# A macaron block's FFN on one Trainium2 core: the mask of picks is transposed by a DMA and multiplied in by VectorE, instead of being added in PSUM by TensorE

## Chip, cores and metric

One Trainium2 chip, one NeuronCore of it. The metric is the time of one execution of the whole program, in microseconds (us): the median of several runs.

## What is computed

The input x is 32 x 512 rows of 256 numbers (16384 rows, 128 tiles of 128 rows). Three layers follow each other, each with a residual: a sparse FFN, an attention layer (gated slot attention), and the same FFN with the same weights again. The change is in the FFN:

```python
lr = xf @ m1                                          # 256 -> 64
mask_logits = jnp.einsum('bl,lxy->bxy', lr, m2) + mb  # 16 groups of 64
quant_mask = jnp.argmax(mask_logits, axis=-1)         # one pick per group
w = w1p[j, quant_mask]
mid = jnp.einsum('ai,aji->aj', xf, w)                 # the picked column of each group
relu = jax.nn.relu(mid)
v = w2p[j, quant_mask]
res = jnp.einsum('ai,aij->aj', relu, v) + b2
x = x + 0.5 * res
```

xf is the layer norm of x. The kernel does not gather weights: it computes all 1024 products of the row, sets those that were not picked to zero, and multiplies all 1024 by w2.

## The kernel before

The program is three phases: FFN, attention, FFN. Each goes over 128 tiles of 128 rows. Every engine has its own hand-written list of stages; a stage comes with an offset, and in step s of a phase the engine does stage (f, o) for tile s + o. So the list of an engine is its order within a step, and instructions of an engine run strictly in that order. The phases overlap by a few steps. The first phase also computes the attention's four projections of x1, the FFN's output (tiles s - 5), and its layer norm (tiles s - 2 and s - 3).

For an FFN tile t the work goes like this (names as in the code, lines of the kernel before):

- VectorE takes the row's mean and variance (L237, L245), GpSimd makes 1/sqrt and x minus mean (`centre`: L249, L254, L256), ScalarE the high f16 half of the normalized row (`high`, L265), VectorE the low half (`low`, L270). Numbers are carried as a high and a low f16 half, and three matmuls stand for one product.
- SP issues the DMA transpose of both halves into `ffn_xT_hl` (`turn`, L281).
- TensorE: `low_rank` makes the 64 low-rank numbers (L472, 6 matmuls of 128 columns), ScalarE (`low_high`, L562 and L563) and VectorE (`low_low`, L628) split them, TensorE's `mask_logits` makes 1024 logits per row, rows on partitions, in banks 1 and 2 (L678, L680).
- VectorE: `first_max` is a running maximum within each group of 64 (L601), `reached` marks the positions where it has reached the group's maximum (L606, into `step`), `reject` compares neighbours of `step` and gives `unpicked`, 1 where a column was not picked, rows on partitions (L615).
- TensorE: `up` makes mid transposed, the 1024 columns on partitions in 8 blocks of 128, rows along the free dimension (L700, 48 matmuls of 128 columns, banks 3 and 4 or 5 and 6). `pick` (L712, 8 matmuls of 128 columns) multiplies `unpicked` by `far_ident`, a diagonal of -2^40, and adds it to the same banks: this transposes the mask and drives what was not picked far below zero.
- ScalarE: `mid_high` is the relu of those banks, rounded to f16 (L556). VectorE: `mid_low` is max(mid, 0) minus that, from PSUM (L622). TensorE: `down` multiplies both halves by w2 (L472, 24 matmuls of 256 columns). VectorE: `finish` adds the residual (L637); GpSimd has added half of b2 to it (`add_bias`, L541); SP stores it (L505).

The orders within a step, with the tile offset in brackets:

```python
# first phase
PE:      up 0, pick 0, project_vf -5, low_rank 2, mask_logits 1, project_qk -5, down -1
VectorE: finish -2, norm.stats 5, norm2.stats -2, low_of_x1 -3, both aggregates, norm.low 4,
         mid_low 0, low_low 2, first_max 1, reached 1, reject 1
ScalarE: norm.high 4, norm2.high -3, mid_high 0, scale_vf -5, low_high 2, swish -5
# third phase
PE:      mask_logits 1, low_rank 2, up 0, pick 0, down -1
VectorE: finish -2, stats 5, low_low 2, first_max 1, reached 1, aggregate 5, low 4, reject 1, mid_low 0
ScalarE: high 4, low_high 2, mid_high 0
```

GpSimd does add_bias -1, centre 5 and, in the first phase, norm2.centre -2. SP issues load 6, load_residual 0, store -2, turn 3 and, in the first phase, norm2.turn -4 and store_projected -6; its queue is in order, and a wait of one entry holds those behind it. `low_of_x1` is norm2's low half, the scalar_tensor_tensor of L270 that writes `att_xn_hl`. The output of `down` and the low-rank numbers share bank 0 in the first phase, so `down` of tile t - 1 also waits for `low_low` of tile t + 2.

## Time and profile before

| | us |
|---|---|
| median of 3 runs | 3081.52 (3077.74 to 3081.72) |
| profiled execution, its own time | 3076.98 |
| span of its profile | 3075.2 |
| TensorE busy | 2976.7 (97% of the span) |
| VectorE busy | 2602.5 (85%) |
| ScalarE busy | 1419.7 (46%) |
| GpSimd busy | 1259.9 (41%) |

Busy time is that of compute instructions. PE is TensorE, DVE is VectorE, ACT is ScalarE, POOL is GpSimd, SPq is SP's queue of DMA issues. In a timeline each line is one instruction (or several of one kind in a row) with its start, its duration and, in square brackets, how long its engine had been idle and for whom. Two instructions in a row of VectorE or ScalarE overlap by about 0.1 us in these lines, so the spacing of starts says what one costs its engine. "PEclk" is the share of full speed that TensorE's clock was granted.

### The profile page before, as it was taken

The page shows a single profiled execution, that of the slowest core. Times are in us where ns is not written, and L with a number is a line of the kernel's source. Part 1 is how long each engine was busy: PE and PEld are TensorE (multiplying, and loading weights), DVE is VectorE, ACT ScalarE, POOL GpSimd, SP SyncE. Part 2 cuts the span into 40 slices and gives each one's busy share as a digit, 9 for nine tenths or more (in the row PEclk, how much of TensorE's full clock was granted, in tenths as well). Part 3 has the DMA queues.
Part 4 walks back from the last instruction along what each step waited for, and adds up shares of the span by engine and source line. Part 5 has one row for each costly group of instructions (what it writes and reads, how often), then busy time and mean ns, then how long its engine had stood idle before and what let it go on. Part 6 is the DMA issues. An engine that isn't in the chain of part 4 may idle for free.

```text
span 3075.2 us, 97305 instructions
## 1 busy us (share of the span) xinstructions
PE 2976.7 (97%) x34688; PEld 2609.5 (85%) x34688; DVE 2602.5 (85%) x4369; ACT 1419.7 (46%) x4051; POOL 1259.9 (41%) x2168
## 2 busy tenths in 40 slices
PE   5999999999999999799999999999899999999999
PEld 4888888888888888688888888888788888888888
DVE  8888888888888887488888888888899999999998
ACT  3333333333333333788888888887222222222222
POOL 4333333333333333255555555555433333333332
PEclk9999999999999999999999999999999999999999
DMA  4444444444444443444444444444332222222222
GB/s 111 119 124 125 125 124 124 124 123 123 123 123 123 123 123 115 126 129 132 133 132 135 133 132 131 131 133 127 92 77 75 75 75 75 76 77 77 76 77 58
DMA packets 485055, 340.86 MB, mean 111 GB/s; under 512 B 301940, under 2 KB 451828, under 8 KB 484984
## 3 DMA queue, kind: packets, MB, share of 16 engines
q1 hardware_dynamic: 484984, 339.91, 39.0%
q8 instruction: 46, 0.75, 0.1%
q14 instruction: 25, 0.20, 0.0%
HBM read 155.19 MB, written 117.44 MB: 89 GB/s over the span
## 4 chain that ended last, share of the span: by engine, by line
PE 93%; issue 2%; DVE 2%; ACT 1%; POOL 0%; DMA 0%; DVEq 0%; SPq 0%; POOLq 0%; ACTq 0%
PE banks L472 37%; PE banks L700 22%; PE banks L1196 7%; PE banks L1167 5%; PE banks L712 4%; PE banks L1192 4%; PE banks L680 3%; PE banks L678 3%; PE banks L1230 3%; PE banks L1157 2%; PE banks L1251 1%; PE banks L1283 1%; DVE masked L1052 1%; PE banks L1245 1%; DVE att_x_out L1134 0%
## 5 line engine op out<-in xcount | busy, mean ns | idle before, releaser
L700 PE MATMUL banks<-ffn_xT_hl,w_hl 128*128 128x128 f16 x12288 | 730.1, 219 | 0.0
L472 PE MATMUL banks<-w_hl,midT_hl 128*128 128x256 f16 x6144 | 712.6, 273 | 6.1 <-DVE low_hl L628 5.5
L700 PEld LDWEIGHTS banks<-ffn_xT_hl,w_hl 128*128 128x128 f16 x12288 | 704.5, 98 | 3.9 <-issue 0.6
L556 ACT ACTIVATE midT_hl<-banks 128x1024 f16<-128x1024 f32 x256 | 261.9, 1023 | 903.8 <-PE banks L712 903.8
L472 PEld LDWEIGHTS banks<-w_hl,midT_hl 128*128 128x128 f16 x6144 | 594.8, 98 | 75.9 <-DVE midT_hl L622 7.3
L249 POOL TENSOR_TENSOR ffn_var_eps<-ffn_moments,eps_col 128x1 f32<-128x1 f32 x256 | 94.1, 367 | 1270.7 <-DVE ffn_moments L245 1270.7
L601 DVE TENSOR_TENSOR_SCAN runmax<-restart,banks 128x1024 f32<-128x1024 f32 x256 | 585.4, 2287 | 8.8 <-PE banks L680 1.0
L622 DVE SCALAR_TENSOR_TENSOR midT_hl<-banks,midT_hl 128x1024 f16<-128x1024 f32 x256 | 312.6, 1221 | 193.8 <-ACT midT_hl L556 193.8
L606 DVE TENSOR_TENSOR step<-runmax 128x1024 bf16<-128x1024 f32 x256 | 314.8, 1230 | 8.9
L472 PE MATMUL banks<-wqkfv_hl,att_xT_hl 128*128 128x512 f16 (+1 forms) x1536 | 292.2, 326 | 1.5 <-DMA att_xT_hl<-att_xn_hl 1.5
L265 ACT ACTIVATE ffn_xn_hl<-ffn_xc,ffn_rstd 128x256 f16<-128x256 f32 x256 | 129.3, 505 | 307.7 <-POOL ffn_xc L256 292.1
L678 PE MATMUL banks<-m_high,low_hl 128*128 128x512 f16 x512 | 195.5, 382 | 2.9 <-DVE runmax L601 1.8
L472 PEld LDWEIGHTS banks<-wqkfv_hl,att_xT_hl 128*128 128x128 f16 x1536 | 139.7, 98 | 68.6 <-DMA att_xT_hl<-att_xn_hl 1.8
L541 POOL TENSOR_TENSOR x_res<-x_res,half_b 128x256 f32<-128x256 f32 x256 | 185.4, 724 | 26.4 <-DMA x_res<-x 25.9
L680 PE MATMUL banks<-m_low_mb,low_h 128*128 128x512 f16 x512 | 195.6, 382 | 0.0
L254 POOL TENSOR_TENSOR ffn_rstd<-ffn_var_eps,minus_half 128x1 f32<-128x1 f32 x256 | 184.1, 719 | 26.9 <-POOL ffn_var_eps L249 13.4
L615 DVE TENSOR_TENSOR unpicked<-step 128x1024 bf16<-128x1024 bf16 x256 | 180.4, 705 | 7.0
L472 PEld LDWEIGHTS banks<-ffn_xT_hl,m_hl 128*128 128x128 f16 x1536 | 107.9, 99 | 84.0 <-ACT w_hl L397 12.9
L994 ACT ACTIVATE prob<-logit,minus_top 128x64 f32<-128x64 f32 x512 | 171.9, 336 | 12.0 <-DVE minus_top L1067 5.1
L573 ACT ACTIVATE qkvf_out<-banks 128x512 f32<-128x512 f32 x128 | 76.5, 598 | 192.2 <-PE banks L472 192.2
L712 PE MATMUL banks<-far_ident,unpicked 128*128 128x128 bf16 x2048 | 156.6, 219 | 4.8 <-DVE unpicked L615 4.8
L1052 DVE TENSOR_TENSOR masked<-banks,causal 128x1024 f32<-128x1024 f32 (+1 forms) x130 | 156.8, 1206 | 0.7 <-PE banks L1167 0.7
(137 smaller groups left out, 5765.2 us busy)
## 6 DMA issues: line engine op xcount, KB each, us to landing
projected<-qkvf_out SPq DMA_DIRECT2D x128, 512.0 KB, 2.9
qkv<-projected SPq DMA_DIRECT2D x128, 384.0 KB, 3.3
x_in<-in_L_attn_x SPq DMA_DIRECT2D x128, 128.0 KB, 2.7
x_res<-in_L_attn_x SPq DMA_DIRECT2D x128, 128.0 KB, 2.1
x<-x_out SPq DMA_DIRECT2D x128, 128.0 KB, 2.0
gate<-projected SPq DMA_DIRECT2D x128, 128.0 KB, 3.1
att_x_res<-x SPq DMA_DIRECT2D x128, 128.0 KB, 2.1
x<-att_x_out SPq DMA_DIRECT2D x128, 128.0 KB, 1.7
```

The costliest lines, as they stand in the source:

```text
L472: last = nc.tensor.matmul(dst, left(lp, k), right(rp, k), start=(k == 0 and lp == rp), stop=(k == blocks - 1 and lp == 1))
L541: nc.gpsimd.tensor_tensor(x_res[:, t.slot], x_res[:, t.slot], half_b2[:, :], ALU.add).then_inc(res_biased, 1)
L556: nc.scalar.activation(midT_hl[:, t.slot, 0], mid_ps[t.slot], ACT.Relu).then_inc(mid_high_made, 1)
L601: nc.vector.tensor_tensor_scan(runmax[:, :], restart[:, :], logits_ps[:, :], FLOOR, ALU.add, ALU.max).then_inc(runmax_made, 1)
L606: nc.vector.tensor_tensor(step[:, :, 1:d2 + 1], groups, groups[:, :, d2 - 1:d2].broadcast_to([P, GROUPS, d2]), ALU.is_equal).then_inc(step ...
L622: nc.vector.scalar_tensor_tensor(midT_hl[:, t.slot, 1], mid_ps[t.slot], 0.0, midT_hl[:, t.slot, 0], ALU.max, ALU.subtract).then_inc(mid_lo ...
L678: nc.tensor.matmul(logits_ps[:, cols], low_hl[:, t.slot], m2_high2[:, cols], start=True, stop=False)
L680: last = nc.tensor.matmul(logits_ps[:, cols], low_h1[:, t.slot], m2_low_mb[:, cols], start=False, stop=True)
L700: nc.tensor.matmul(mid_ps[t.slot][:, cols], w1_hl[:, wp, k, cols], xT_hl[:, t.ring, xp, k], start=(c % PER_BANK == 0 and k == 0 and wp == xp),
L712: last = nc.tensor.matmul(mid_ps[t.slot][:, cols], unpicked[:, t.slot, cols], far_ident[:, :], start=False, stop=True, skip_group_check=True)
L1052: nc.vector.tensor_tensor(masked[:, t.slot, :, which].rearrange("p z b (a t) -> p z (b a) t", a=PAIRS), pair_ps[:, :, which].rearrange("p ...
L1196: last = nc.tensor.matmul(dst[:, at:at + HD], inner[:, z, a * P:(a + 1) * P], right[:, at:at + HD], start=(t.chunk == 0), stop=True, skip_ ...
```

## The change

`pick`, `far_ident` and `unpicked` go. `reject` becomes `pick_first`, which makes `picked` (1 where a column is picked) for the same tile. A new stage of SP, `turn_picked`, transposes it by DMA: 128 x 1024 bf16 into `pickedT`, 8 blocks of 128 x 128, where `turn` does 4. A new stage of VectorE, `cut`, makes `mid_cut` = max(mid, 0) * pickedT, 1024 columns of f32 in SBUF. `mid_high` becomes a copy of `mid_cut` to f16 on ScalarE, and `mid_low` (mid_cut minus its high half) moves from VectorE to GpSimd, at offset -1 and first in GpSimd's step. `up` raises `up_done`, for which `turn` of tile t + 4 and `cut` wait.

```diff
+                def turn_picked(t):
+                    if isinstance(t.n, int):
+                        after(sp, picked_made, t)
+                        after(sp, cut_made, t, lag=2)
+                    sp.dma_start_transpose(pickedT[:, t.slot], picked[:, t.slot]).then_inc(pick_turned[t.slot], 16)
...
-                              (load_residual, 0), (store, -2),
-                              (lambda t: norm.turn(sp, t, mid_picked), 3), (first_only(load_down, sp), 3),
+                              (load_residual, 0), (store, -2), (turn_picked, 0),
+                              (lambda t: norm.turn(sp, t, up_done), 3), (first_only(load_down, sp), 3),
...
-                              (lambda t: norm.turn(sp, t, mid_picked), 3)]
+                              (turn_picked, 0), (lambda t: norm.turn(sp, t, up_done), 3)]
...
-                stages = [(add_bias, -1), (lambda t: norm.centre(pool, t), 5)]
+                def mid_low(t):
+                    after(pool, mid_high_made, t)
+                    nc.gpsimd.tensor_tensor(midT_hl[:, t.slot, 1].rearrange("p c t -> p (c t)"), mid_cut[:, t.slot],
+                                            midT_hl[:, t.slot, 0].rearrange("p c t -> p (c t)"),
+                                            ALU.subtract).then_inc(mid_low_made, 1)
+                stages = [(mid_low, MID_LOW), (add_bias, -1), (lambda t: norm.centre(pool, t), 5)]
...
                 def mid_high(t):
-                    after(act, mid_picked, t)
+                    after(act, cut_made, t)
                     after(act, res_done, t, lag=2)
-                    nc.scalar.activation(midT_hl[:, t.slot, 0], mid_ps[t.slot], ACT.Relu
-                                         ).then_inc(mid_high_made, 1)
+                    nc.scalar.activation(midT_hl[:, t.slot, 0].rearrange("p c t -> p (c t)"), mid_cut[:, t.slot],
+                                         ACT.Copy).then_inc(mid_high_made, 1)
...
-                              (mid_high, 0), (scale_vf, -5), (low_high, 2), (first_only(round_down, act), 2),
-                              (swish, -5), (first_only(round_attention, act), -1)]
+                              (scale_vf, -5), (low_high, 2), (first_only(round_down, act), 2),
+                              (swish, -5), (mid_high, 0), (first_only(round_attention, act), -1)]
...
-                def reject(t):
+                def pick_first(t):
                     after(dve, step_made, t)
-                    after(dve, mid_picked, t, lag=2)
+                    after_dma(dve, pick_turned, t, lag=2)
                     nc.vector.tensor_tensor(
-                        unpicked[:, t.slot].rearrange("p (g d) -> p g d", g=GROUPS),
+                        picked[:, t.slot].rearrange("p (g d) -> p g d", g=GROUPS),
                         step[:, :, 0:d2], step[:, :, 1:d2 + 1],
-                        ALU.is_ge).then_inc(unpicked_made, 1)
-
-                def mid_low(t):
-                    after(dve, mid_high_made, t)
-                    nc.vector.scalar_tensor_tensor(midT_hl[:, t.slot, 1], mid_ps[t.slot], 0.0,
-                                                   midT_hl[:, t.slot, 0], ALU.max,
-                                                   ALU.subtract).then_inc(mid_low_made, 1)
+                        ALU.is_lt).then_inc(picked_made, 1)
+
+                def cut(t):
+                    after(dve, up_done, t)
+                    after_dma(dve, pick_turned, t)
+                    after(dve, mid_low_made, t, lag=2)
+                    nc.vector.scalar_tensor_tensor(mid_cut[:, t.slot], mid_ps[t.slot], 0.0,
+                                                   pickedT[:, t.slot].rearrange("p c t -> p (c t)"), ALU.max,
+                                                   ALU.mult).then_inc(cut_made, 1)
...
-                              (first_only(rest_of_up, dve), 3), (mid_low, 0), (low_low, 2), (first_max, 1),
-                              (reached, 1), (reject, 1), (first_only(rest_of_down, dve), 1),
+                              (first_only(rest_of_up, dve), 3), (low_low, 2), (first_max, 1),
+                              (reached, 1), (cut, 0), (pick_first, 1), (first_only(rest_of_down, dve), 1),
...
-                          (lambda t: norm.low(dve, t), 4), (reject, 1), (mid_low, 0)]
+                          (lambda t: norm.low(dve, t), 4), (cut, 0), (pick_first, 1)]
...
-                    after(pe, mid_low_made, t, lag=2)
+                    after(pe, cut_made, t, lag=2)
...
-                    stages = [(up, 0), (pick, 0), (project_vf, -5), (low_rank, 2), (mask_logits, 1),
+                    stages = [(up, 0), (project_vf, -5), (low_rank, 2), (mask_logits, 1),
                               (project_qk, -5), (down, -1)]
                 else:
-                    stages = [(mask_logits, 1), (low_rank, 2), (up, 0), (pick, 0), (down, -1)]
+                    stages = [(mask_logits, 1), (low_rank, 2), (up, 0), (down, -1)]
```

ScalarE in the first phase's loop, before (`mid_high` is L556, `swish` L573, `scale_vf` L581, `low_high` L562 and L563):

```order
L265 ACTIVATE att_xn_hl<-att_xc,att_rstd 128x256 [waits att_xT_turned2]
L556 ACTIVATE midT_hl<-banks 128x1024 [waits res_done,mid_picked]
L57 ISA [waits vf_projected]
L581 ACTIVATE qkvf_out<-banks 128x512 [waits qkvf_stored0]
L562 ACTIVATE low_hl<-banks 128x128 [waits logits_done,low_done]
L563 ACTIVATE low_h<-banks 64x128
L573 ACTIVATE qkvf_out<-banks 128x512 [waits qk_projected]
```

The same place in the changed kernel (its lines: `high` L263, `scale_vf` L590, `low_high` L571 and L572, `swish` L582, `mid_high` L565):

```order
L263 ACTIVATE att_xn_hl<-att_xc,att_rstd 128x256 [waits att_xT_turned2]
L57 ISA [waits vf_projected]
L590 ACTIVATE qkvf_out<-banks 128x512 [waits qkvf_stored0]
L571 ACTIVATE low_hl<-banks 128x128 [waits logits_done,low_done]
L572 ACTIVATE low_h<-banks 64x128
L582 ACTIVATE qkvf_out<-banks 128x512 [waits qk_projected]
L565 ACTIVATE midT_hl<-mid_cut 128x1024 [waits res_done,cut_made]
```

`mid_high` has moved from near the step's start to its end, and waits for VectorE's `cut` instead of TensorE.

VectorE in the third phase's loop, before, from `reached` (L606) to the next step's `low_low` (L628):

```order
L606 TENSOR_TENSOR step<-runmax 128x16x64 [waits runmax_made]
L245 BN_AGGR ffn_moments<-ffn_stats 128x2
L51 REGISTER_ALU
L270 SCALAR_TENSOR_TENSOR ffn_xn_hl<-ffn_xc,ffn_rstd,ffn_xn_hl 128x256 [waits ffn_xn_high_made]
L615 TENSOR_TENSOR unpicked<-step 128x1024 [waits mid_picked,step_made]
L622 SCALAR_TENSOR_TENSOR midT_hl<-banks,midT_hl 128x1024 [waits mid_high_made]
L637 SCALAR_TENSOR_TENSOR x_out<-banks,x_res 128x256 [waits out_stored1,res_biased,res_done]
L57 ISA [waits ffn_var_eps_made,ffn_centred]
L237 BN_STATS ffn_stats<-x_in 128x6 [waits ffn_x_loaded0]
L628 TENSOR_TENSOR low_hl<-banks,low_hl 64x128 [waits low_high_made]
```

The same in the changed kernel (`reached` L615, `cut` L633, `pick_first` L624, `finish` L648, `low_low` L639):

```order
L615 TENSOR_TENSOR step<-runmax 128x16x64 [waits runmax_made]
L243 BN_AGGR ffn_moments<-ffn_stats 128x2
L51 REGISTER_ALU
L268 SCALAR_TENSOR_TENSOR ffn_xn_hl<-ffn_xc,ffn_rstd,ffn_xn_hl 128x256 [waits ffn_xn_high_made]
L633 SCALAR_TENSOR_TENSOR mid_cut<-banks,pickedT 128x1024 [waits mid_low_made,pick_turned0,up_done]
L624 TENSOR_TENSOR picked<-step 128x1024 [waits pick_turned1,step_made]
L648 SCALAR_TENSOR_TENSOR x_out<-banks,x_res 128x256 [waits out_stored1,res_biased,res_done]
L57 ISA [waits ffn_var_eps_made,ffn_centred]
L235 BN_STATS ffn_stats<-x_in 128x6 [waits ffn_x_loaded0]
L639 TENSOR_TENSOR low_hl<-banks,low_hl 64x128 [waits low_high_made]
```

`cut` stands where `reject` stood, `pick_first` where `mid_low` stood; `cut` waits for a DMA, and what comes after it on ScalarE is given in the list of stages above: high 4, low_high 2, mid_high 0, unchanged in this phase.

## Rows read from the trace of the kernel before

**Rows 1.** The page, part 1: busy us, share of the span, instructions.
```profile
PE 2976.7 (97%) x34688; PEld 2609.5 (85%) x34688; DVE 2602.5 (85%) x4369; ACT 1419.7 (46%) x4051; POOL 1259.9 (41%) x2168
```

**Rows 2.** Windows view: stretches of the first and the third phase.
```profile
core 0: us, PE busy (x) PEld busy (x) DVE busy (x) ACT busy (x) POOL busy (x), PEclk, DMA share, GB/s
100.00:1100.00 1000.00, 1000.00 (x11929) 840.70 (x11928) 811.65 (x1258) 348.95 (x730) 365.36 (x733) 1.00 0.43 123
2250.00:3050.00 800.00, 800.00 (x10363) 713.85 (x10362) 769.47 (x1033) 223.53 (x459) 284.64 (x458) 1.00 0.28 75
```

**Rows 3.** Timeline of the first phase: start us, us, then the instruction.
```profile
801.08 0.61 PE L712 MATMUL banks<-far_ident,unpicked 128*128 128x128 bf16 x8
...
804.11 0.29 DVE L628 TENSOR_TENSOR low_hl<-banks,low_hl 64x128 f16<-64x128 f32 x1
804.44 2.29 DVE L601 TENSOR_TENSOR_SCAN runmax<-restart,banks 128x1024 f32<-128x1024 f32 x1
...
806.03 0.50 ACT L265 ACTIVATE ffn_xn_hl<-ffn_xc,ffn_rstd 128x256 f16<-128x256 f32 x1
806.43 0.50 ACT L265 ACTIVATE att_xn_hl<-att_xc,att_rstd 128x256 f16<-128x256 f32 x1
806.76 1.23 DVE L606 TENSOR_TENSOR step<-runmax 128x1024 bf16<-128x1024 f32 x1
...
810.64 0.61 PE L712 MATMUL banks<-far_ident,unpicked 128*128 128x128 bf16 x8
```

**Rows 4.** Timeline of the attention phase: GpSimd and VectorE side by side.
```profile
1803.76 0.73 POOL L919 TENSOR_TENSOR Pt<-prob,expG 128x256 f32<-128x256 f32 x1 [0.31 <-ACT prob L994]
...
1804.06 0.72 DVE L1126 TENSOR_TENSOR o_hl<-o_norm,o_hl 128x256 f16<-128x256 f32 x1
...
1804.45 0.85 POOL L900 TENSOR_TENSOR gate_hl<-logsig,gate_hl 128x256 f16<-128x256 f32 x1
...
1804.90 0.68 DVE L1036 SCALAR_TENSOR_TENSOR St<-keep,expnG 128x256 f32<-128x256 f32 x1
...
1808.32 1.01 POOL L928 TENSOR_TENSOR o_rms<-o_sum_eps,minus_half 128x4 f32<-128x4 f32 x1
...
1808.98 0.43 DVE L1027 SCALAR_TENSOR_TENSOR logsig<-gate,lnone 128x256 f32<-128x256 f32 x1 [0.23 <-ACT lnone L951]
```

**Rows 5.** Source view of the attention's GpSimd lines: ns min/median/max.
```profile
L900 POOL TENSOR_TENSOR gate_hl<-logsig,gate_hl x128: 664/673/859, 1249.1 to 2136.8; 128x256 f16<-128x256 f32 x128
L924 POOL TENSOR_TENSOR o_sum_eps<-o_sum,eps_sum_col x128: 196/198/203, 1296.4 to 2170.9; 128x4 f32<-128x4 f32 x128
```

**Rows 6.** Timeline of the third phase, one step and the next one's start.
```profile
2605.95 0.42 DVE L637 SCALAR_TENSOR_TENSOR x_out<-banks,x_res 128x256 f32<-128x256 f32 x1
...
2606.89 0.29 DVE L628 TENSOR_TENSOR low_hl<-banks,low_hl 64x128 f16<-64x128 f32 x1 [0.19 <-ACT low_hl L562]
...
2607.51 1.19 SPq L281 DMA_TRANSPOSE ffn_xT_hl<-ffn_xn_hl  x1
...
2609.71 1.02 ACT L556 ACTIVATE midT_hl<-banks 128x1024 f16<-128x1024 f32 x1 [2.69 <-PE banks L712]
...
2611.15 0.70 DVE L615 TENSOR_TENSOR unpicked<-step 128x1024 bf16<-128x1024 bf16 x1
...
2611.77 1.22 DVE L622 SCALAR_TENSOR_TENSOR midT_hl<-banks,midT_hl 128x1024 f16<-128x1024 f32 x1
...
2612.90 0.41 DVE L637 SCALAR_TENSOR_TENSOR x_out<-banks,x_res 128x256 f32<-128x256 f32 x1
...
2613.00 0.51 ACT L265 ACTIVATE ffn_xn_hl<-ffn_xc,ffn_rstd 128x256 f16<-128x256 f32 x1 [2.27 <-POOL ffn_xc L256]
...
2613.53 0.28 ACT L562 ACTIVATE low_hl<-banks 128x128 f16<-128x128 f32 x1
...
2613.84 0.29 DVE L628 TENSOR_TENSOR low_hl<-banks,low_hl 64x128 f16<-64x128 f32 x1 [0.19 <-ACT low_hl L562]
```

**Rows 7.** Tile view of ffn_xT_hl, 2300 to 3050 us: its transposes' landing.
```profile
DMA to landing us min/median/max: 2.4/2.6/4.0
```

More of the change, by code:

```diff
@@ L125, in build @@
     FLOOR = -3.0e38
-    FAR_BELOW = -(2.0 ** 40)
     S_ATT = 64.0
@@ L155, in bank @@
             return banks[:, first * BANK:(first + count) * BANK]
-        far_ident = sb("far_ident", [P, P], bf16)
         w1_hl = sb("w1_hl", [P, 2, KD, d_ff], f16)
@@ L185, in build @@
         runmax = sb("runmax", [P, d_ff])
-        unpicked = sb("unpicked", [P, 2, d_ff], bf16)
+        picked = sb("picked", [P, 2, d_ff], bf16)
+        pickedT = sb("pickedT", [P, 2, KF, P], bf16)
+        mid_cut = sb("mid_cut", [P, 2, KF * P])
         midT_hl = sb("midT_hl", [P, 2, 2, KF, P], f16)
@@ L699, in up @@
                             for wp, xp in ((0, 0), (0, 1), (1, 0)):
-                                nc.tensor.matmul(mid_ps[t.slot][:, cols], w1_hl[:, wp, k, cols],
-                                                 xT_hl[:, t.ring, xp, k],
-                                                 start=(c % PER_BANK == 0 and k == 0 and wp == xp),
-                                                 stop=False, skip_group_check=True)
-                def pick(t):
-                    if is_first(t) and in_first:
-                        pe.wait_ge(ident_made, 1)
-                    after(pe, unpicked_made, t)
-                    for c in range(KF):
-                        cols = slice(c * P, (c + 1) * P)
-                        last = nc.tensor.matmul(mid_ps[t.slot][:, cols], unpicked[:, t.slot, cols],
-                                                far_ident[:, :], start=False, stop=True,
-                                                skip_group_check=True)
-                    last.then_inc(mid_picked, 1)
+                                last = nc.tensor.matmul(mid_ps[t.slot][:, cols], w1_hl[:, wp, k, cols],
+                                                        xT_hl[:, t.ring, xp, k],
+                                                        start=(c % PER_BANK == 0 and k == 0 and wp == xp),
+                                                        stop=(c % PER_BANK == PER_BANK - 1 and k == KD - 1
+                                                              and wp == 1), skip_group_check=True)
+                    last.then_inc(up_done, 1)
                 def low_rank(t):
@@ L1172, in products_A @@
                     if is_first(t):
-                        pe.wait_ge(mid_low_made, tiles)
+                        pe.wait_ge(cut_made, tiles)
                     after(pe, S["T_made"], t)
```

12 lines of the change are left out of this document (4 added, 8 removed).

## The prediction, made before the changed kernel ran

> **What bounds the kernel now.** I read the page first: TensorE is busy 97% of the span, VectorE 85%, GpSimd 41% [rows 1]. Shares are averages, so I took windows of the first and the third phase next [rows 2]. In the first TensorE is never idle, VectorE is busy 81% and GpSimd 37%. In the third TensorE is never idle either, but VectorE is at 96% (769.47 of 800). The clock granted is 1.00 in both, the upper of its two levels (2.4 GHz). The timelines give the periods, the time from one tile to the next: 9.56 us in the first phase, from one `pick` to the next (810.64 - 801.08) [rows 3], and 6.95 us in the third, from one `finish` to the next (2612.90 - 2605.95) [rows 6]. Both phases run 128 tiles; the attention between them is not changed. So the question is only how these two periods change, and each 0.1 us of period is 12.8 us of time.
>
> **TensorE's part.** Eight matmuls of 128 columns go, 0.61 us from the first's start to the last's recorded end [rows 3]. Recorded ends overlap the next start: eight at about 0.055 us each, start to start, are 0.45 us. If TensorE stayed the bound, the periods would be 9.11 and 6.50. Everything else asks whether somebody else can keep up.
>
> **VectorE's own work** stays the same. `pick_first` is `reject` with another comparison. `cut` takes one operand from PSUM and one from SBUF over 1024 columns, as `mid_low` did: 1.22 us, and 1.13 from its start to the next one's (2612.90 - 2611.77) [rows 6]. Only the wait of 0.19 before `low_low` in the third phase could go [rows 6]: 6.95 less 0.19 and some 0.06 is 6.70. That is a floor for the third phase, above TensorE's 6.50.
>
> **New in the third phase: a ring through ScalarE.** Before, `mid_high` waited for TensorE only and sat idle 2.69 us for it [rows 6]. Now it waits for `cut`, which is last but one in VectorE's step, and behind it in ScalarE's queue stand the next step's `high` and `low_high`, for which VectorE's next `low_low` waits. From a `low_low` around to the next:
> - `low_low` to the place of `reject`, now `cut`: 2611.15 - 2606.89 = 4.26 [rows 6]
> - `cut` 1.22 and a semaphore, 0.05: 1.27
> - `mid_high`: 1.02 [rows 6], plus 0.02 chosen for an SBUF source, less 0.10 of overlap with the next: 0.94
> - `high` to `low_high`: 0.40 (806.43 - 806.03) [rows 3]
> - `low_high` to `low_low`: 0.31 (2613.84 - 2613.53) [rows 6]
>
> The sum is 7.18, 0.23 over today's period.
>
> **A second ring there, through the DMA.** SP issues `turn_picked` behind the store, which waits for `finish`. Today SP reaches that place 1.56 us after `finish` starts (2607.51 - 2605.95) [rows 6]. The landing of 8 blocks is in no row. Bounds: 2.6 us as 4 blocks take [rows 7], if more blocks cost nothing, and 5.2, twice that. I take 3.8: a transpose of four blocks holds SP 1.19 [rows 6], and a second one issued right behind would land 1.2 after the first. Then `cut` starts 1.56 + 3.8 + 0.05 = 5.41 after `finish`, `pick_first` 1.13 later, and the next `finish` the 0.62 that `reject` took after that (2611.77 - 2611.15) [rows 6]: 7.16. The two rings tie. I take 7.20 for the third phase: + 0.25 x 128 = **+32 us**. A rule of the Trainium skill speaks harder against the change: VectorE: DVE Perf Modes, section on the three transpose paths, has one 128 x 128 bf16 block at 1309 ns by DMA and 390 on TensorE. Eight in a row would be an estimated 10.5 us by that page, a period of 13.9 and some 890 us more; but four blocks that land in 2.6 us are already faster than it says.
>
> **New in the first phase: GpSimd holds VectorE.** The attention phase shows it [rows 4]. `o_hl` (L1126, two operands in SBUF) starts at 1803.76 + 0.30 while GpSimd's L919 runs to 1804.49; it takes 0.72 and ends 0.29 after GpSimd has. L1036 starts under L900, which runs to 1805.30, and ends 0.28 after it. So a VectorE instruction with two SBUF operands waits for the end of a GpSimd instruction that streams a tile. The Trainium skill (SBUF — State Buffer, SBUF: two separate sides) calls that pair of ports an exclusive lock, held for the whole instruction. The whole of it does not hold here: L1027 ran its 0.43 us under the pow of L928, 1.01 us on 4 columns [rows 4]. But a subtraction over 1024 columns streams all along.
>
> What does `mid_low` cost on GpSimd? The same subtraction on 256 columns takes 0.673 and an addition on 4 columns 0.198 [rows 5]; the line through both gives 0.20 + 1020 x 0.00188 = 2.1 us. Four times 0.673 is the upper end, 2.7, and 2.0 the lower. I take 2.1, since the fixed part is seen. By the GPSIMD Engine Reference, section 3.1 (4497 ns for 2048 columns of f32), an estimate is 2.25 us, and the sum below would be 19 us more.
>
> The ring, from `cut`'s start: `cut` 1.22 + 0.05, `mid_high` 1.04 + 0.05, `mid_low` 2.1, which starts 2.36 after `cut` did. `low_of_x1` has two SBUF operands and can't start before ScalarE has done `high` and `norm2.high` behind `mid_high` (1.27 + 0.94 + 0.40 + 0.50 + 0.05 = 3.16), so it always finds `mid_low` running. It ends 0.29 after it; then `add_bias` takes its turn (about 0.6 more), and `norm.low`, two SBUF operands too, ends after that: `low_low` can start 1.15 after `mid_low`'s end. Then `low_low` to the scan 0.33, the scan 2.32, `reached` 1.14 (1.23 less the overlap) [rows 3]. The sum is 9.40, between TensorE's 9.11 and today's 9.56: -0.16 x 128 = **-20 us**. Of the 58 us that TensorE would give back, 38 are eaten. The DMA has room here: `turn_picked` lands about 7 us after `cut` began, over 2 before it is needed. The other transposes come 2.4 us later in SP's queue; SP issues some 6 us in a step of 9.4. Nothing else waits for them that early.
>
> **Ends.** At the end of each FFN phase nothing covers the last tile: 3.8 of DMA for 0.45 of TensorE and about 0.9 more for `mid_low`, some 4 us twice: **+8 us**. Less work on GpSimd at the start (`far_ident`) is under 1 us.
>
> **Sum.** 3077 (the profiled execution) - 20 + 32 + 8 = 3097. The median of the runs is 4.5 above that execution, so I predict 3102 for the median, 0.7% slower. About 0.2% (6 us) is what a measurement of this kernel can tell from no change.
>
> **Rivals.**
> - *GpSimd does not hold VectorE for long, and the first phase gets what TensorE gives up.* For it: the pow that held nobody [rows 4]; against it: L1126 and L1036 in the same rows. Period 9.11, -58 in place of -20: 3064, **faster**. It decides from a `mid_low` or a hold under 1.8 us. Chance 0.20.
> - *`mid_low` costs four times the short one*, 2.7 us. First phase 10.0, +55: 3177. For it: GpSimd instructions run longer when VectorE is in their way (L900 0.85 for 0.67 [rows 4, 5]). Chance 0.13.
> - *The transpose of 8 blocks lands later than 4 us*, because blocks add up fully or because it meets the others in the queue (single landings reach 4.0 already [rows 7]). VectorE then stands before `cut` in the third phase, each 0.1 us costing 12.8. At 4.5 us: period 7.86, 3186; at 5.2: 3276. Chance 0.15.
> - *Neither ring closes*: overlaps larger than I took, and VectorE's own 6.70 is the third phase's period. -58 - 32 + 8: 3000. Chance 0.05.
>
> The forecast has 0.47, with a range of its own of 3080 to 3135 (the hold's 2.0 to 2.3 us, 7.1 to 7.35 in the third phase). The range 3055 to 3185 adds the first two rivals and the near half of the third, and leaves out the far half and the last. Faster by over 0.2%: 0.20 + 0.05 and 0.04 of the forecast's low end, 0.29. Within 0.2%: 0.07. Slower: 0.64.
>
> **What the profile after would show.** TensorE with gaps in both phases, about 0.3 us per tile in the first and 0.7 in the third, with VectorE or ScalarE as releasers. `low_of_x1`'s scalar_tensor_tensor near 1.7 us where `norm.low`'s other uses take 0.45. In the third phase, a wait of `low_low` for ScalarE of about 0.4 in place of 0.19, or a wait of `cut` for the DMA of pickedT: which of the two says which ring was longer. Windows of 100 to 1000 us and of the third phase give the periods: 9.4 and 7.2. I am wrong if the first phase's period is 9.1, or if the third's is under 7.0.

## The result and the profile after

The changed kernel takes 3115.16 us (median; 3113.04 to 3116.45, 4 runs), the kernel before 3081.62 on the same occasions (3077.74 to 3082.57, 4 runs). The ratio is 1.0111, with a 95% interval of 1.0093 to 1.0128: 1.1% slower. The prediction was 3102, in a range of 3055 to 3185, with 0.64 on slower.

The page, part 1, of the changed kernel:

```profile
PE 2909.8 (93%) x32640; PEld 2490.0 (80%) x32640; DVE 2768.3 (89%) x4369; ACT 1402.2 (45%) x4051; POOL 1781.5 (57%) x2422
```

TensorE is recorded busy for 67 us less than in [rows 1], and is now idle for 7% of the span. VectorE is recorded busy for 166 us more, though it has as many instructions (4369) of the same sizes. That is the first sign that some of them are held while they run. The same two stretches as in [rows 2]:

```profile
100.00:1100.00 1000.00, 974.39 (x11132) 790.48 (x11132) 944.66 (x1261) 353.64 (x736) 601.94 (x841) 1.00 0.57 152
2250.00:3050.00 800.00, 742.18 (x9122) 639.63 (x9120) 753.67 (x1001) 197.25 (x445) 476.85 (x557) 1.00 0.47 110
```

In the first phase VectorE went from 81% to 94%, and TensorE has gaps: 0.24 us a tile, in which it waits for `low_low` before `down`. In the third TensorE has gaps of 0.52 us a tile, mostly waiting for GpSimd's `mid_low`, and VectorE has some too: 94% where it had 96%. The clock is 1.00 in both as before.

For periods I count scans, one per tile, in equal windows of both kernels (source view, min/median/max of the duration, then the first and the last start). This is the changed kernel, 100 to 1100 us and 2300 to 2950 us:

```profile
L610 DVE TENSOR_TENSOR_SCAN runmax<-restart,banks x106: 2286/2287/2289, 99.8 to 1099.7; 128x1024 f32<-128x1024 f32 x106
L610 DVE TENSOR_TENSOR_SCAN runmax<-restart,banks x91: 2286/2287/2290, 2301.5 to 2948.3; 128x1024 f32<-128x1024 f32 x91
```

999.9 / 105 = 9.52 us in the first phase and 646.8 / 90 = 7.19 in the third. The kernel before has 985.2 / 103 = 9.565 and 645.8 / 93 = 6.944 in the same windows. The span grew by 3112.4 - 3075.2 = 37.2 us. Of these the first phase gives 128 x (9.523 - 9.565) = -5, the third 128 x (7.187 - 6.944) = +31, and the rest, +11, lies in the ends of the phases and the attention between them. From the first scan of a phase to its last (127 periods, its slower start and end included) it is -4 in the first and +35 in the third, with 7 left outside.

**First phase, the ring through GpSimd** (timeline; `cut` is L633, `mid_high` L565, `mid_low` L549, L263 is `high` and `norm2.high`, L268 `low_of_x1` and `norm.low`, L543 `add_bias`):

```profile
799.71 1.06 ACT L565 ACTIVATE midT_hl<-mid_cut 128x1024 f16<-128x1024 f32 x1 [4.25 <-DVE mid_cut L633]
...
800.67 0.49 ACT L263 ACTIVATE ffn_xn_hl<-ffn_xc,ffn_rstd 128x256 f16<-128x256 f32 x1
...
800.84 2.13 POOL L549 TENSOR_TENSOR midT_hl<-mid_cut,midT_hl 128x1024 f16<-128x1024 f32 x1 [3.52 <-ACT midT_hl L565]
801.07 0.49 ACT L263 ACTIVATE att_xn_hl<-att_xc,att_rstd 128x256 f16<-128x256 f32 x1
...
801.70 1.55 DVE L268 SCALAR_TENSOR_TENSOR att_xn_hl<-att_xc,att_rstd,att_xn_hl 128x256 f16<-128x256 f32 x1 [0.50 <-ACT att_xn_hl L263]
...
802.92 0.91 POOL L543 TENSOR_TENSOR x_res<-x_res,half_b 128x256 f32<-128x256 f32 x1
...
803.33 0.79 DVE L268 SCALAR_TENSOR_TENSOR ffn_xn_hl<-ffn_xc,ffn_rstd,ffn_xn_hl 128x256 f16<-128x256 f32 x1
...
804.15 0.29 DVE L639 TENSOR_TENSOR low_hl<-banks,low_hl 64x128 f16<-64x128 f32 x1
...
804.48 2.29 DVE L610 TENSOR_TENSOR_SCAN runmax<-restart,banks 128x1024 f32<-128x1024 f32 x1
...
806.80 1.23 DVE L615 TENSOR_TENSOR step<-runmax 128x1024 bf16<-128x1024 f32 x1
...
807.94 1.22 DVE L633 SCALAR_TENSOR_TENSOR mid_cut<-banks,pickedT 128x1024 f32<-128x1024 f32 x1
...
809.27 1.06 ACT L565 ACTIVATE midT_hl<-mid_cut 128x1024 f16<-128x1024 f32 x1 [4.33 <-DVE mid_cut L633]
```

`mid_high` starts 9.56 us apart (799.71, 809.27); the steps of this phase take 9.48 to 9.57. `mid_low` runs from 800.84 to 802.97. `low_of_x1`, due at 801.70, takes 1.55 us instead of the 0.48 to 0.49 it took before and ends at 803.25, 0.28 after `mid_low`. Then `add_bias` takes its turn, 0.91 instead of 0.72, to 803.83, and `norm.low`, which started at 803.33, ends 0.29 after that. It is the pattern of [rows 4], with a GpSimd instruction three times as long.

**Third phase, the ring through ScalarE** (timeline, a step and the next `cut`; L571 is `low_high`, L639 `low_low`, L507 `turn_picked`):

```profile
2701.05 1.22 DVE L633 SCALAR_TENSOR_TENSOR mid_cut<-banks,pickedT 128x1024 f32<-128x1024 f32 x1
...
2702.31 1.06 ACT L565 ACTIVATE midT_hl<-mid_cut 128x1024 f16<-128x1024 f32 x1 [5.38 <-DVE mid_cut L633]
...
2703.27 0.49 ACT L263 ACTIVATE ffn_xn_hl<-ffn_xc,ffn_rstd 128x256 f16<-128x256 f32 x1
...
2703.67 0.26 ACT L571 ACTIVATE low_hl<-banks 128x128 f16<-128x128 f32 x1
...
2703.96 0.29 DVE L639 TENSOR_TENSOR low_hl<-banks,low_hl 64x128 f16<-64x128 f32 x1 [0.33 <-ACT low_hl L571]
...
2704.28 2.29 DVE L610 TENSOR_TENSOR_SCAN runmax<-restart,banks 128x1024 f32<-128x1024 f32 x1
2704.40 1.24 SPq L507 DMA_TRANSPOSE pickedT<-picked  x1
...
2706.61 1.23 DVE L615 TENSOR_TENSOR step<-runmax 128x1024 bf16<-128x1024 f32 x1
...
2708.21 1.22 DVE L633 SCALAR_TENSOR_TENSOR mid_cut<-banks,pickedT 128x1024 f32<-128x1024 f32 x1
```

From one `low_low` to the next `cut` 4.25 us, then `cut`, `mid_high`, `high`, `low_high` one behind the other, and `low_low` waits 0.33 us for ScalarE, as against 0.19 in [rows 6]. SP issues the transpose of the mask at 2704.40, in 1.24 us for 8 blocks, where 4 blocks took 1.19 in [rows 6]. The landing of the 8 blocks (tile view of pickedT, 2300 to 3050 us):

```profile
DMA to landing us min/median/max: 3.1/3.3/5.0
```

So it is there at 2707.7 (2704.40 + 3.3), half a microsecond ahead of `cut` at 2708.21. The chain of waits tells another story for the same stretch (start, us, what):

```profile
2696.59 0.38 SPq L499
2697.02 3.33 DMA pickedT<-picked
2701.05 1.23 DVE mid_cut L633
2702.42 0.21 issue
```

It names the DMA of pickedT on the critical chain, 9% of the whole span. But that landing was over at 2700.35 and `cut` started at 2701.05. A chain puts a wait down to the last release that it sees, and where two rings are within a microsecond of each other it may walk along the wrong one. Experiment 1 was made to tell them apart.

### The profile page after: what moved, and what is told of

It reads as the page before. It is cut to its first block, busy times and chain, and to the rows that moved or that the text cites. A ratio compares the mean times of both kernels' runs of the same rounds, so it can differ in the third digit from the quotient of the medians.

```text
span 3112.4 us, 94106 instructions
## 1 busy us (share of the span) xinstructions
PE 2909.8 (93%) x32640; PEld 2490.0 (80%) x32640; DVE 2768.3 (89%) x4369; ACT 1402.2 (45%) x4051; POOL 1781.5 (57%) x2422
## 4 chain that ended last, share of the span: by engine, by line
DVE 33%; PE 27%; issue 19%; DMA 10%; ACT 5%; SPq 2%; POOL 2%; DVEq 1%; ACTq 1%; POOLq 0%
DVE runmax L610 11%; DMA pickedT<-picked 9%; PE banks L1197 7%; DVE mid_cut L633 6%; PE banks L1168 5%; DVE att_xn_hl L268 5%; PE banks L465 4%; PE banks L1193 3%; DVE ffn_xn_hl L268 3%; PE banks L1231 3%; ACT ffn_xn_hl L263 2%; PE banks L1158 2%; DVE picked L624 2%; ACT att_xn_hl L263 2%; DVE low_hl L639 1%
## 5 line engine op out<-in xcount | busy, mean ns | idle before, releaser
L549 POOL TENSOR_TENSOR midT_hl<-mid_cut,midT_hl 128x1024 f16<-128x1024 f32 x256 | 547.0, 2137 | 605.0 <-ACT midT_hl L565 604.9
L565 ACT ACTIVATE midT_hl<-mid_cut 128x1024 f16<-128x1024 f32 x256 | 270.6, 1057 | 1241.9 <-DVE mid_cut L633 1241.9
L465 PEld LDWEIGHTS banks<-w_hl,midT_hl 128*128 128x128 f16 x6144 | 584.6, 98 | 225.2 <-POOL midT_hl L549 88.9
L633 DVE SCALAR_TENSOR_TENSOR mid_cut<-banks,pickedT 128x1024 f32<-128x1024 f32 x256 | 312.0, 1219 | 13.2 <-issue 11.9
L615 DVE TENSOR_TENSOR step<-runmax 128x1024 bf16<-128x1024 f32 x256 | 314.4, 1228 | 8.9
L268 DVE SCALAR_TENSOR_TENSOR att_xn_hl<-att_xc,att_rstd,att_xn_hl 128x256 f16<-128x256 f32 x128 | 200.6, 1567 | 53.3 <-ACT att_xn_hl L263 52.9
L247 POOL TENSOR_TENSOR ffn_var_eps<-ffn_moments,eps_col 128x1 f32<-128x1 f32 x256 | 89.5, 350 | 249.8 <-DVE ffn_moments L243 249.8
L543 POOL TENSOR_TENSOR x_res<-x_res,half_b 128x256 f32<-128x256 f32 x256 | 210.0, 820 | 0.0
L624 DVE TENSOR_TENSOR picked<-step 128x1024 bf16<-128x1024 bf16 x256 | 189.4, 740 | 0.0
L925 POOL TENSOR_TENSOR o_sum_eps<-o_sum,eps_sum_col 128x4 f32<-128x4 f32 x128 | 25.4, 199 | 282.4 <-DVE o_sum L1122 282.3
L582 ACT ACTIVATE qkvf_out<-banks 128x512 f32<-128x512 f32 x128 | 76.4, 597 | 192.0 <-PE banks L465 192.0
L268 DVE SCALAR_TENSOR_TENSOR ffn_xn_hl<-ffn_xc,ffn_rstd,ffn_xn_hl 128x256 f16<-128x256 f32 x256 | 156.6, 612 | 4.3 <-ACT ffn_xn_hl L263 4.3
```

The costliest lines, as they stand in the source:

```text
L268: nc.vector.scalar_tensor_tensor(self.xn_hl[:, t.slot, 1], self.xc[:, t.slot], self.rstd[:, t.slot], self.xn_hl[:, t.slot, 0], ALU.mult, A ...
L465: last = nc.tensor.matmul(dst, left(lp, k), right(rp, k), start=(k == 0 and lp == rp), stop=(k == blocks - 1 and lp == 1))
L543: nc.gpsimd.tensor_tensor(x_res[:, t.slot], x_res[:, t.slot], half_b2[:, :], ALU.add).then_inc(res_biased, 1)
L549: nc.gpsimd.tensor_tensor(midT_hl[:, t.slot, 1].rearrange("p c t -> p (c t)"), mid_cut[:, t.slot], midT_hl[:, t.slot, 0].rearrange("p c t ...
L565: nc.scalar.activation(midT_hl[:, t.slot, 0].rearrange("p c t -> p (c t)"), mid_cut[:, t.slot], ACT.Copy).then_inc(mid_high_made, 1)
L615: nc.vector.tensor_tensor(step[:, :, 1:d2 + 1], groups, groups[:, :, d2 - 1:d2].broadcast_to([P, GROUPS, d2]), ALU.is_equal).then_inc(step ...
```

## Experiments

All ran beside the kernel before. Its medians there were 3080.32 (experiments 1 to 4, on one chip), 3079.76 (5 to 8, on a second) and 3078.56 (9 and 10, on a third). The changed kernel itself was not run again beside them: differences from its 3115.16 compare across occasions on which the kernel before differed by 1 to 3 us. Periods are from scans counted as above. The theory: two rings, one in each phase; the hold by `mid_low` in the first, ScalarE's order in the third. The rivals: the transposing DMA is what is late; or the first phase is slow because `mid_low` comes late for `down`, hold or not; or TensorE's share was never worth anything.

**1. ScalarE's order in the third phase.**

```diff
-                return Phase([high, (low_high, 2), (mid_high, 0)], tiles, base, UNROLL, LONGEST_LAG, starts_at)
+                return Phase([(low_high, 2), high, (mid_high, 0)], tiles, base, UNROLL, LONGEST_LAG, starts_at)
```

> The changed kernel, but in the third phase ScalarE does low_high ahead of high (low_high 2, high 4, mid_high 0). Ring through ScalarE: low_low no longer waits for high, so the third phase's period falls by 0.40 us from 7.18 to about 6.8, the first phase's stays 9.53; 3115 - 0.38 x 128 = about 3066 us. Ring through the DMA: pickedT is what is late, the order on ScalarE changes nothing, 7.18 and 3115 us. If VectorE's idle time before low_low just moves elsewhere (the share of the lock), between the two.

Measured: 3082.47 us (ratio to the kernel before 1.0009, 0.9999 to 1.0019), 33 us under the changed kernel. The first phase's period is 9.52, unchanged; the third's is 647.4 / 94 = 6.89, 0.30 less. Timeline of its third phase:

```profile
2605.47 1.22 DVE L633 SCALAR_TENSOR_TENSOR mid_cut<-banks,pickedT 128x1024 f32<-128x1024 f32 x1
...
2606.72 1.06 ACT L565 ACTIVATE midT_hl<-mid_cut 128x1024 f16<-128x1024 f32 x1 [5.08 <-DVE mid_cut L633]
...
2607.68 0.26 ACT L571 ACTIVATE low_hl<-banks 128x128 f16<-128x128 f32 x1
...
2608.00 0.50 ACT L263 ACTIVATE ffn_xn_hl<-ffn_xc,ffn_rstd 128x256 f16<-128x256 f32 x1
2608.07 0.29 DVE L639 TENSOR_TENSOR low_hl<-banks,low_hl 64x128 f16<-64x128 f32 x1
```

`low_high` now stands ahead of `high`, and `low_low` waits for nobody. The DMA is issued in the same place of SP's list as before, so it was not what held the period at 7.19. The gain is 0.30 and not 0.40 because VectorE is next: it is busy 639.63 of 650 us (98%), 6.78 us a tile.

**2. mid_low beside the scan, in the first phase.**

```diff
                     after(pool, mid_high_made, t)
+                    if in_first:
+                        after(pool, norm.low_made, t, lag=-5)
```

> The changed kernel, but in the first phase GpSimd's mid_low of tile t also waits for VectorE's norm.low of tile t + 5, so that it runs beside the scan and not in front of the two instructions with two SBUF operands. If GpSimd's hold on VectorE makes the first phase's ring: low_of_x1 back to 0.49 us from 1.55, period 9.53 to 9.1 or 9.2 (TensorE's 9.11), although mid_low is now later by 1.5 us; 3115 - 0.37 x 128 = about 3068 us. If the first phase is bound by how late mid_low and what follows from it are, a later mid_low makes the period longer, 9.8 or more, 3150 us or more. Third phase 7.18 in both.

Measured: 3083.39 us (1.0012, 1.0002 to 1.0021). First phase 989.3 / 107 = 9.25, third 7.17. `low_of_x1` is back at 0.485 us (median) and `norm.low` at 0.452. A wait was added to a kernel that has too many, `mid_low` starts later against `cut` than before (4.4 us after it instead of 2.4, medians), and the kernel is 32 us faster. What is left to TensorE's 9.11 has two candidates that were not taken apart. The weight loads of `down` are late in every second step (54 of 108), and TensorE is recorded idle before `down` in 28 steps, 0.24 us each: it waits for this later `mid_low`. And GpSimd's subtraction of the mean holds VectorE's `reached` in 40 of 109 cases, for up to 1.68 us instead of 1.23.

**3. Both.**

> Both edits of the two kernels before in one. If the two rings are the two causes, each in its own phase, the gains add: 9.15 and 6.8, about 3115 - 49 - 47 = 3020 us, 2% below the kernel before. If one cause serves both phases, the second edit adds little: 3065 us.

Measured: 3049.06 us (0.9903, 0.9886 to 0.9919), 66 us under the changed kernel: 33 and 32 add up. Periods 9.25 and 6.88. Expected was 3020; both single edits had given about 15 us less than expected, the first because VectorE is next in line, the second for the 0.13 us a tile that were left to TensorE's 9.11.

**4. The kernel before without pick.**

```diff
-                    stages = [(up, 0), (pick, 0), (project_vf, -5), (low_rank, 2), (mask_logits, 1),
+                    stages = [(up, 0), (project_vf, -5), (low_rank, 2), (mask_logits, 1),
...
-                    stages = [(mask_logits, 1), (low_rank, 2), (up, 0), (pick, 0), (down, -1)]
+                    stages = [(mask_logits, 1), (low_rank, 2), (up, 0), (down, -1)]
```

with the semaphore of `pick` raised by the last matmul of `up`.

> The kernel before, with pick left out and nothing in its place: the mask is made but not applied, so all 1024 columns of mid are used. What TensorE's 0.45 us per tile is worth when nobody else gets slower: first phase 9.56 to 9.11, -58 us; third phase 6.95 to between 6.70 (VectorE's own work) and 6.9 (VectorE still waits for ScalarE's low_high), -6 to -32 us; 2990 to 3020 us. If TensorE was not the bound in the first phase, no change there.

Measured: 3007.13 us (0.9764, 0.9748 to 0.9780). First phase 994.0 / 109 = 9.12, third 646.9 / 95 = 6.81. So TensorE's eight matmuls are worth 0.45 us a tile in the first phase and 0.13 in the third, where VectorE takes over as the bound. That is all that could be won by taking them off TensorE with the engines' lists as they stand: 73 us.

**5. Half of mid_low.** On GpSimd only the columns 0 to 511; the low half of the others is set to zero once, at the start.

```diff
-                    nc.gpsimd.tensor_tensor(midT_hl[:, t.slot, 1].rearrange("p c t -> p (c t)"), mid_cut[:, t.slot],
-                                            midT_hl[:, t.slot, 0].rearrange("p c t -> p (c t)"),
+                    nc.gpsimd.tensor_tensor(midT_hl[:, t.slot, 1, 0:KF // 2].rearrange("p c t -> p (c t)"),
+                                            mid_cut[:, t.slot, 0:KF // 2 * P],
+                                            midT_hl[:, t.slot, 0, 0:KF // 2].rearrange("p c t -> p (c t)"),
                                             ALU.subtract).then_inc(mid_low_made, 1)
```

> The changed kernel, with mid_low on only the first half of the columns: the low f16 half of mid stays zero for the other 512. mid_low falls from 2.13 to about 1.2 us. Ring through GpSimd's hold: the first phase's period falls by up to 0.9 but not under TensorE's 9.11, so 9.52 to 9.1 to 9.2; the third phase does not change (7.18), since mid_low is not in its ring; about 3115 - 50 = 3065 us. If mid_low's length is nothing to the first phase, 3115; if it is also in the third phase's ring, well under 3060.

Measured: 3064.72 us (0.9950, 0.9933 to 0.9966). Source view, first phase:

```profile
L268 DVE SCALAR_TENSOR_TENSOR att_xn_hl<-att_xc,att_rstd,att_xn_hl x110: 572/576/690, 101.8 to 1095.9; 128x256 f16<-128x256 f32 x110
...
L550 POOL TENSOR_TENSOR midT_hl<-mid_cut,midT_hl x110: 1155/1158/1162, 101.1 to 1095.1; 128x512 f16<-128x512 f32 x110
```

`mid_low` is 0.97 shorter, so is `low_of_x1` (0.576 for 1.55), and the period is 9.12, TensorE's own. `norm.low` is still held by `add_bias` (0.78), which now costs nothing. The third phase stays at 7.18: there, `mid_low`'s length is not in the ring.

**6. The held instructions moved, mid_low left alone.** In the first phase VectorE does `low_of_x1` and `norm.low` behind the scan; the aggregates stand ahead of it, and `low_low` takes over the wait for the statistics.

```diff
-                              (lambda t: norm2.stats(dve, t, out_made), -2), (low_of_x1, -3),
+                              (lambda t: norm2.stats(dve, t, out_made), -2),
...
-                              (first_only(rest_of_up, dve), 3), (low_low, 2), (first_max, 1),
-                              (reached, 1), (cut, 0), (pick_first, 1), (first_only(rest_of_down, dve), 1),
+                              (first_only(rest_of_up, dve), 3), (low_low, 2),
+                              (lambda t: norm.aggregate(dve, t), 5), (lambda t: norm2.aggregate(dve, t), -2),
+                              (first_max, 1),
+                              (low_of_x1, -3), (lambda t: norm.low(dve, t), 4), (reached, 1), (cut, 0), (pick_first, 1), (first_only(rest_of_down, dve), 1),
```

> The changed kernel, but in the first phase VectorE does low_of_x1 and norm.low behind the scan instead of ahead of it; GpSimd's order and mid_low's time are as they were. If the hold makes the ring, low_of_x1 (1.55 us) and norm.low (0.79) no longer stand beside mid_low and fall back to 0.49 and 0.45 unless they meet GpSimd's short ones, and the period is 9.1 to 9.4; 3062 to 3100 us. If the period hangs on how late mid_low ends (TensorE's down), it stays at 9.52 and 3115 us, since mid_low ends no earlier.

Measured: 3072.68 us (0.9977, 0.9968 to 0.9987); periods 9.12 and 7.18. Source view of its first phase:

```profile
L268 DVE SCALAR_TENSOR_TENSOR att_xn_hl<-att_xc,att_rstd,att_xn_hl x110: 457/459/463, 104.1 to 1098.2; 128x256 f16<-128x256 f32 x110
L268 DVE SCALAR_TENSOR_TENSOR ffn_xn_hl<-ffn_xc,ffn_rstd,ffn_xn_hl x110: 474/480/862, 104.5 to 1098.6; 128x256 f16<-128x256 f32 x110
```

GpSimd is as slow as it was (`mid_low` 2.130 us), and TensorE has its 9.12. With experiments 2 and 5 this leaves no room for the rival of the late `mid_low`: a later one, a shorter one, and the same one with other neighbours all free the phase. The time is 8 us above experiment 5's at the same two periods; it was lost outside the steady steps, and why is open.

**7. The mask transposed twice.** A transpose into a tile that nobody reads goes ahead of the one that is used; `pick_first` waits for this one as well before it overwrites `picked`.

```diff
+                    sp.dma_start_transpose(spare[:, t.slot], picked[:, t.slot]).then_inc(spare_turned[t.slot], 16)
                     sp.dma_start_transpose(pickedT[:, t.slot], picked[:, t.slot]).then_inc(pick_turned[t.slot], 16)
```

> The changed kernel, with a second transpose of the same mask, into a tile that nobody reads, issued ahead of the one that is used, in both phases. pickedT lands 1.23 us later at least (one more issue), 1.6 if the data of 8 blocks counts too. Third phase: the ring through the DMA is 1.5 + 3.3 + 0.05 + 1.13 + 0.7 = 6.7 us and 0.5 under the one through ScalarE, so it comes on top by 0.7 to 1.1: period 7.9 to 8.3. First phase: over 2 us of room, no change, 9.52. Total 3205 to 3260 us. If the third phase already hangs on the DMA, +1.2 to 1.6 there: 3270 to 3320 us; if the DMA has room everywhere, 3115.

Measured: 3221.92 us (1.0460, 1.0439 to 1.0481). First phase 991.1 / 104 = 9.53, unchanged; third 641.2 / 81 = 7.92. VectorE's waits in the third phase:

```profile
DVE mid_cut L636 <- issue: 41.5, 62, 1.7
DVE low_hl L642 <- ACT low_hl L573: 34.5, 82, 0.5
DVE mid_cut L636 <- DMA pickedT<-picked: 12.0, 20, 0.8
```

`cut` now waits in every step: in 20 the profile names the landing, in the 62 put down to "issue" it names no releaser. Here the DMA's ring is the longer one. The extra issue puts the used one 1.28 us later:

```profile
2607.20 1.24 SPq L508 DMA_TRANSPOSE spare<-picked  x1
...
2608.48 1.32 SPq L509 DMA_TRANSPOSE pickedT<-picked  x1
```

It lands in 3.3 us (median) as before. With the extra issue the ring is 7.92, so without it it is 6.64, an estimate by this difference: the DMA's ring in the changed kernel is over 0.5 shorter than the 7.19 that ScalarE's ring makes.

**8. high ahead of mid_high, in the first phase of experiment 3.**

```diff
                     stages = [high, (first_only(round_up, act), 3), (lambda t: norm2.high(act, t), -3),
-                              (scale_vf, -5), (low_high, 2), (first_only(round_down, act), 2),
-                              (swish, -5), (mid_high, 0), (first_only(round_attention, act), -1)]
+                              (mid_high, -1), (scale_vf, -5), (low_high, 2), (first_only(round_down, act), 2),
+                              (swish, -5), (first_only(round_attention, act), -1)]
```

> e3_both, and in the first phase ScalarE does high and norm2.high of the next step ahead of mid_high, so that VectorE's low_of_x1 and norm.low, and with them mid_low, come 0.3 us earlier. In e3_both TensorE still waits 0.2 to 0.3 us for mid_low in every second step (period 9.25). If that is all that keeps it from 9.11: 3049 - 0.13 x 128 = 3032 us. If the collisions of GpSimd's short instructions with VectorE's reached make the rest, no gain: 3049 us.

Measured: 3039.98 us (0.9869, 0.9853 to 0.9886). First phase 991.1 / 108 = 9.18, third 6.88. About half of what was left to TensorE's 9.11 came. `reached` is still held in this phase, for 1.37 us on average instead of 1.23; whether that makes the rest is not shown.

**9. Experiments 6 and 1 together.**

> e6_lows_behind_scan in the first phase (9.12, TensorE's own bound) and e1_low_high_first in the third (6.89). If the two are independent: 3072.7 - 0.30 x 128 = about 3034 us, 1.4 to 1.5% below the kernel before and level with or a little under e8 (3040). If the 8 us that e6 lost at the ends of its phases against e5 come from the third phase's start, they may change too: 3026 to 3045 us.

Measured: 3038.11 us (0.9867, 0.9850 to 0.9883). Periods 9.12 and 6.89. Level with experiment 8 within what can be told. Both beat the kernel before by 1.3%: the change pays once the two rings are open. The kernel before was not run with a changed order of its own; TensorE is never idle in either of its phases [rows 2], so a new order of the other engines should give it little, but no run shows this.

**10. mid_low back on VectorE**, ahead of the scan in both phases, as a subtraction of two SBUF operands.

```diff
-                    nc.gpsimd.tensor_tensor(midT_hl[:, t.slot, 1].rearrange("p c t -> p (c t)"), mid_cut[:, t.slot],
...
+                    nc.vector.tensor_tensor(midT_hl[:, t.slot, 1].rearrange("p c t -> p (c t)"), mid_cut[:, t.slot],
...
-                              (first_only(rest_of_up, dve), 3), (low_low, 2), (first_max, 1),
+                              (first_only(rest_of_up, dve), 3), (mid_low, MID_LOW), (low_low, 2), (first_max, 1),
...
-                stages = [(finish, -2), (lambda t: norm.stats(dve, t), 5), (low_low, 2), (first_max, 1),
+                stages = [(finish, -2), (lambda t: norm.stats(dve, t), 5), (low_low, 2), (mid_low, MID_LOW), (first_max, 1),
```

> The changed kernel with mid_low taken back by VectorE (mid_cut minus its high half, both from SBUF, 1.2 us), ahead of the scan in both phases, so that only the transposing by DMA and the multiplication are left of the change. First phase: no hold, VectorE's work is 7.7 + 1.13 = 8.8 us, period 9.11 (TensorE) to 9.3. Third phase: VectorE has 6.70 + 1.13 = 7.8 us, and the ring through ScalarE passes mid_low too, 7.18 + 1.13 = 8.3. Total 3115 - 0.3 x 128 + 1.1 x 128 = about 3215 us. If the hold were not the first phase's cause, that phase stays at 9.5 or grows with VectorE's work: 3250 us.

Measured: 3264.76 us (1.0607, 1.0587 to 1.0626). Third phase 640.8 / 76 = 8.43, near the 8.3 expected. The first phase is a miss: 994.7 / 105 = 9.47, not 9.11 to 9.3. Timeline of its first phase (L247 is the variance plus eps, one column; L632 `mid_low`, L608 `reached`, L626 `cut`, L543 `add_bias`):

```profile
797.11 1.22 DVE L626 SCALAR_TENSOR_TENSOR mid_cut<-banks,pickedT 128x1024 f32<-128x1024 f32 x1
...
800.44 0.48 DVE L268 SCALAR_TENSOR_TENSOR att_xn_hl<-att_xc,att_rstd,att_xn_hl 128x256 f16<-128x256 f32 x1 [0.50 <-ACT att_xn_hl L263]
...
801.00 0.46 DVE L268 SCALAR_TENSOR_TENSOR ffn_xn_hl<-ffn_xc,ffn_rstd,ffn_xn_hl 128x256 f16<-128x256 f32 x1
801.10 1.55 POOL L247 TENSOR_TENSOR ffn_var_eps<-ffn_moments,eps_col 128x1 f32<-128x1 f32 x1 [3.31 <-DVE ffn_moments L243]
...
801.37 1.22 DVE L632 TENSOR_TENSOR midT_hl<-mid_cut,midT_hl 128x1024 f16<-128x1024 f32 x1
...
805.27 1.23 DVE L608 TENSOR_TENSOR step<-runmax 128x1024 bf16<-128x1024 f32 x1
805.33 1.75 POOL L543 TENSOR_TENSOR x_res<-x_res,half_b 128x256 f32<-128x256 f32 x1
...
806.41 1.22 DVE L626 SCALAR_TENSOR_TENSOR mid_cut<-banks,pickedT 128x1024 f32<-128x1024 f32 x1
```

The hold is gone from `low_of_x1` (0.48). But it waits 0.50 us for ScalarE, whose `norm2.high` stands behind `mid_high` and `cut`. So the first phase has a ring of its own through ScalarE. In the step shown it runs from `cut` at 797.11 to the next at 806.41, 9.30 us: 3.33 to `low_of_x1`, and 5.97 from there, of which `mid_low` is 1.25. Over the window the first part is 3.26 on average and the ring 9.23, inside the 9.11 to 9.3 expected, as long as `reached` takes its 1.23. It often doesn't (its source view, first phase, and another step):

```profile
L608 DVE TENSOR_TENSOR step<-runmax x106: 1227/1437/1712, 103.6 to 1098.3; 128x1024 bf16<-128x1024 f32 x106
```

```profile
776.57 0.73 POOL L543 TENSOR_TENSOR x_res<-x_res,half_b 128x256 f32<-128x256 f32 x1
776.67 1.71 DVE L608 TENSOR_TENSOR step<-runmax 128x1024 bf16<-128x1024 f32 x1
```

In 64 of 106 steps `add_bias` starts just ahead of `reached` (two operands in SBUF) and holds it, for 1.43 to 1.71 us; in the other 42 `reached` starts first, takes 1.23, and `add_bias` is the one that lasts, 1.75 instead of 0.72. On average `reached` is 0.24 longer, and 9.23 + 0.24 is the 9.47 measured. So the miss is a hold that the expectation had not counted, by a short GpSimd instruction that now stands beside `reached`. The stretch shows the hold the other way round once more: GpSimd's sum over one column takes 1.55 us under `norm.low` and `mid_low`, where a sum of the same shape takes 0.19 beside the scan, and 0.34 to 0.40 beside `norm.low` alone in the kernel before.

## Why the prediction was right

Sign, mechanism and place were right in both phases; the size was short by 13 us (3102 for 3115). Term by term:

- *TensorE's part*, 0.45 us a tile: 9.565 - 9.119 = 0.45 in experiment 4. Right, and the floor of 9.11 too.
- *VectorE's own work unchanged*: `cut` takes 1.219 us, as reckoned, `pick_first` 0.70 when it is not held. In the third phase it meets GpSimd's subtraction of the mean and takes 0.79 (mean), so the work is not quite unchanged. The floor of 6.70 was too low in itself: without the wait before `low_low`, VectorE's starts in the kernel before follow each other in 6.78 (6.95 less 0.17; nothing gives the further 0.06). Experiment 4, with the same work for VectorE but no `mid_low` on GpSimd, stops at 6.81, and experiments 1 and 9, with the longer `pick_first`, at 6.89.
- *Third phase, +32 us*: +31. The ring through ScalarE was put at 7.18 and is 7.19, and its five terms are right too: 4.26, 1.27, 0.96, 0.40 and 0.29 on average, for 4.26, 1.27, 0.94, 0.40 and 0.31. Experiment 1 shows that it is this ring. `mid_high` from SBUF takes 1.057 us (0.03 more than from PSUM; 0.02 was taken).
- *The second ring there* was sized wrong, without harm. I took 3.8 us for the landing of 8 blocks, by one more issue of 1.2. SP needs 1.23 us for 8 blocks, no more than for 4 (1.28 in the same kernel), and they land in 3.3: 0.7 more than 4 blocks. The ring is about 6.64 and not 7.16 (experiment 7). The two rings do not tie. The 7.20 that was forecast holds by the ring through ScalarE alone; that the mis-sized ring agreed with it was chance.
- *First phase, -20 us*: -5. This is the term that was mis-sized. The ring was put at 9.40 and is 9.52 on average. `mid_low` was taken at 2.10 and is 2.13. It starts 2.42 us after `cut`, not 2.36: `mid_high` waits 0.07 and not 0.05 after `cut`'s end, `mid_low` 0.08 after `mid_high`'s, and `mid_high` is 0.02 longer. From `mid_low`'s end to `low_low` are 1.18 and not 1.15. Together these are 0.12 us, or some 15 us in 128 tiles. The other three terms (0.33, 2.32, 1.14) are as reckoned.
- *Ends, +8 us*: +11.
- *From the profile to the median, +4.5 us*: +0.6 (3114.53 to 3115.16). The profiled execution is 17 us above the forecast of 3097, the median 13 above that of 3102; the offset of one fast profile of the kernel before hid 4.
- *The rivals.* GpSimd does not hold VectorE: false, by experiments 2, 5 and 6. `mid_low` at four times the short one, 2.7: false, 2.13; the line through two rows was right. The landing beyond 4 us: false in the median (3.3; single ones reach 5.0). Neither ring closes: false.
- *The signs to look for.* TensorE's gaps are 0.24 and 0.52 us a tile, for 0.3 and 0.7, and the releaser in the third phase is mostly GpSimd's `mid_low`, which was not named; experiment 5 shows that this wait does not make the period. `low_of_x1` takes 1.55 and not 1.7, and `low_low` waits 0.33 and not 0.4.

By the figure of the Trainium skill's GPSIMD Engine Reference, section 3.1, `mid_low` would be an estimated 2.25 us; 2.13 was measured (with an f16 operand and an f16 result). The rule of the Trainium skill's SBUF — State Buffer (SBUF: two separate sides), an exclusive lock, agrees with `low_of_x1` ending 0.28 us after `mid_low`. The Trainium skill's 1309 ns for one 128 x 128 bf16 block by DMA (VectorE: DVE Perf Modes, the three transpose paths) does not carry over to a transpose of 8 blocks in one DMA: 3.3 us landing, 0.41 a block.
